# A fused two-layer kernel: the attention of the first layer in another order of work

## The chip, the cores and the metric

The kernel runs on one core of a Trainium2 chip. The metric is the device time of one execution in microseconds (us): lower is better. Engines are named PE (TensorE, the matmuls; PEld are its weight loads), DVE (VectorE), ACT (ScalarE), POOL (GpSimd) and SP (the queue that issues most transfers).

## The reference, cut to what matters

The input is x of 4 batches x 512 rows x 128. Layer 0 is attention and a mixture of experts, layer 1 a gated linear recurrence with its feed-forward parts. Each part reads the rows normalised to mean 0 and variance 1 and is added to them. The change touches attention, and of the tail its residual, norm and choice of experts:

```python
Q, K, V = (heads(WQ), heads(WK), heads(WV))          # 16 heads of 8
score = jnp.einsum('bhqd,bhkd->bhqk', Q, K) / jnp.sqrt(jnp.asarray(D_K, x.dtype))
score = score + mask                                 # causal
score = score - jnp.max(score, axis=-1, keepdims=True)
score = jnp.exp(score)
score = score / jnp.sum(score, axis=-1, keepdims=True)
out = jnp.einsum('bhqk,bhkd->bhqd', score, V)
out = out.transpose(0, 2, 1, 3).reshape(B, S, E)
return out @ WO
...
probs_full = jax.nn.softmax(xt @ Wr, axis=-1)        # 8 experts
topv, topi = jax.lax.top_k(probs_full, TOPK)         # 2 of them for each row
topv = topv / jnp.sum(topv, axis=-1, keepdims=True)
onehot = jax.nn.one_hot(topi, E, dtype=x.dtype)
rank = jnp.cumsum(onehot, axis=0)
keep = (rank <= capacity).astype(x.dtype) * onehot
...
x = x + _L0_attn_ref(_layernorm(x, axis=-1), L0_attn_WQ, L0_attn_WK, L0_attn_WV, L0_attn_WO)
x = x + _L0_ffn_ref(_layernorm(x, axis=-1), L0_ffn_Wr, L0_ffn_W1, L0_ffn_b1, L0_ffn_W2, L0_ffn_b2)
```

## The kernel before, in words

Attention works on groups of four heads of one batch: 4 batches (b) x 4 groups (g) are 16 groups, and loop step w treats group w. The lines are those of the functions printed below.

**Row scores.** To subtract a maximum, each group's scores are first computed with queries on the partitions: `row_scores(G, u)` makes ten blocks u of 128 queries x (4 heads x 128 keys) into three PSUM banks used in turn (`RING`, `row_free`); blocks 1, 4, 5 and 9 lie on the diagonal and take a second matmul that adds the mask. DVE's `row_max` reduces each (L1074) and so frees its bank. `minus_max` joins them and writes minus the maximum into two columns of MX for each head and tile (L1080 to L1082). PE turns MX (`turn_max`, L1687) and DVE adds it to the queries (`add_max`, L1088): QM.

**Key scores.** `key_scores(w, n)`, n = 0 to 11 (head n % 4; n // 4 is key tile 0, tile 1, or tiles 2 and 3) gives scores with keys on the partitions, the maximum already in them, in three more banks. ACT's `exp_unit` (L684) writes their exponentials to PT and frees the bank; POOL's `select` (L551) zeroes what is above the diagonal. `values(w, j)` multiplies key tile j with V, four heads on 32 columns of the array each (L1673), into bank 6. When all four tiles are in, ACT copies bank 6 to OG (`store_sums`, L691), PE turns it (`turn_out`, L1695) and DVE divides by the sums (`normalise`, L1096, L1097).

**One step.** Step w interleaves the row scores of group w + 1, the key scores of group w and the rest of group w - 1: key scores 10 and 11 and the values of tiles 1 (first visit), 2 and 3 (second visit); values(w, 0) are a third visit. Row scores 0 and 1 of group w + 2 come at the end of the step, ahead of the turned maxima of group w + 1. Key scores 8 and 9 of group w come before that turn. Each engine's order is written out by hand in its own block; all turns and small products share bank 7 in the order of `TURNS`.

**Queries and keys through DRAM.** They are held as a high and a low part in four planes of 8 rows (three products make up for single-precision ones; the fourth plane carries the maxima). When g = 0, PE makes the projections of batch b + 1 (`project`, L1632, L1633) in the ring banks, ACT rounds them (`round_halves`, L674), DVE takes the low parts (`make_halves`, L1064), and SP writes the planes to `qk_dram` (`store_planes`, six transfers) and loads them per group (`pad`: QS once, KP in four transfers, L409 and L418). Plane 4 is constant and stored ahead (`store_pads`, L384, L386). In DRAM a head is 4 planes x 8 rows.

**The tail of a batch** runs in the four steps of the next batch: heads turned (g = 0, L1701, ACT copy L702), product with WO, residual, mean and variance, POOL's root, normalisation on DVE (g = 1, L1707, L1110, L979 to L991), second turn and router logits (g = 2, L1715, L1721), choice of two experts (`choose`, `spread`, L1130 to L1144), ranks by matmul (g = 3), places and counts (`place`, `count`, L1159 to L1171). POOL scatters the normed rows to the experts' slots in DRAM (L537). The tail of the last batch stands by itself after the loop, in halves. The experts and layer 1 follow; the change leaves them as they are.

## Time and profile before

| | |
|---|---|
| median of 3 runs | 651.49 us (650.28 to 654.68) |
| the profiled execution | 651.65 us, of which the span from first to last instruction is 649.9 |
| PE busy | 577.0 us (89%), 3423 matmuls |
| PE weight loads | 440.7 us (68%) |
| DVE busy | 407.6 us (63%), 966 instructions |
| ACT busy | 325.8 us (50%), 567 |
| POOL busy | 172.5 us (27%), 185 |
| clock granted to PE | 0.964 of full speed in the mean |
| DRAM | 25.12 MB read, 16.78 MB written |
| chain that ended last | PE 62%, DVE 11%, issue 8%, ACT 6%, DMA 6% |

Matmuls overlap and their ends are modelled, so a busy PE is read by the starts of its instructions. The 16 attention steps take 27.8 to 209.7 us of the span, the experts about 236 to 320, layer 1 the rest.

### The profile page before, as it was taken

The page shows a single profiled execution, that of the slowest core. Times are in us where ns is not written, and L with a number is a line of the kernel's source. Part 1 is how long each engine was busy: PE and PEld are TensorE (multiplying, and loading weights), DVE is VectorE, ACT ScalarE, POOL GpSimd, SP SyncE. Part 2 cuts the span into 40 slices and gives each one's busy share as a digit, 9 for nine tenths or more (in the row PEclk, how much of TensorE's full clock was granted, in tenths as well). Part 3 has the DMA queues.
Part 4 walks back from the last instruction along what each step waited for, and adds up shares of the span by engine and source line. Part 5 has one row for each costly group of instructions (what it writes and reads, how often), then busy time and mean ns, then how long its engine had stood idle before and what let it go on. Part 6 is the DMA issues. An engine that isn't in the chain of part 4 may idle for free.

```text
span 649.9 us, 9448 instructions
## 1 busy us (share of the span) xinstructions
PE 577.0 (89%) x3423; PEld 440.7 (68%) x3423; DVE 407.6 (63%) x966; ACT 325.8 (50%) x567; POOL 172.5 (27%) x185
## 2 busy tenths in 40 slices
PE   7889989999998479979558688999999999998997
PEld 3556656556565369979435476678778878786866
DVE  6778688788885522533249986983769556762430
ACT  5756556556656116636216344752575256643451
POOL 6112122452542630000158623611300041001100
PEclk9999999999999679989879898999999999999999
DMA  4773242243110444764101100100000000000000
GB/s 131 229 252 105 75 131 66 82 146 98 54 45 2 133 148 128 211 204 126 48 25 32 29 6 1 33 1 1 1 18 1 0 1 18 0 1 2 17 1 16
DMA packets 44926, 42.51 MB, mean 65 GB/s; under 512 B 4176, under 2 KB 34384, under 8 KB 44880
## 3 DMA queue, kind: packets, MB, share of 16 engines
q1 hardware_dynamic: 42544, 37.44, 19.1%
q0 software_dynamic: 2048, 4.20, 2.2%
q8 instruction: 27, 0.44, 0.3%
q10 hardware_dynamic: 288, 0.28, 0.2%
q14 instruction: 19, 0.16, 0.1%
HBM read 25.12 MB, written 16.78 MB: 64 GB/s over the span
## 4 chain that ended last, share of the span: by engine, by line
PE 62%; DVE 11%; issue 8%; ACT 6%; DMA 6%; SPq 3%; POOL 2%; DVEq 0%; ACTq 0%; POOLq 0%
PE ps L1992 7%; PE ps L1645 5%; PE ps L1661 5%; PE ps L1673 5%; PE ps L2014 5%; PE ps L2095 4%; PE ps L2091 4%; PE ps L2092 4%; PE ps L1930 4%; PE ps L2015 4%; PE ps L2018 4%; DMA XS<-xs_dram 3%; PE ps L2008 2%; DVE pm L1074 2%; PE ps L1648 2%
## 5 line engine op out<-in xcount | busy, mean ns | idle before, releaser
L684 ACT ACTIVATE PT<-ps 128x384 f32<-128x384 f32 (+1 forms) x192 | 93.5, 529 | 69.6 <-PE ps L1661 65.0
L1074 DVE TENSOR_REDUCE pm<-ps 128x4 f32<-128x512 f32 x160 | 102.4, 683 | 10.0 <-PE ps L1645 9.4
L1645 PE MATMUL ps<-KP,QS 128*128 128x512 f32 x160 | 71.7, 452 | 7.7 <-DVEq L1067 2.5
L551 POOL TENSOR_SCALAR_AFFINE_SELECT PT<-PT 128x512 f32<-128x512 f32 x64 | 40.1, 638 | 128.0 <-ACT PT L684 126.6
L1661 PE MATMUL ps<-QM,KP 128*128 128x512 f32 (+3 forms) x256 | 69.2, 331 | 1.5 <-DVE QM L1088 1.1
L1661 PEld LDWEIGHTS ps<-QM,KP 128*128 128x128 f32 x256 | 43.8, 189 | 22.8 <-issue 13.4
L1645 PEld LDWEIGHTS ps<-KP,QS 128*128 128x128 f32 x160 | 29.8, 188 | 27.2 <-DVE pm L1074 10.7
L1444 DVE TENSOR_TENSOR_SCAN zero<-decay,OG 128x512 f32<-128x512 f32 x32 | 44.8, 1401 | 1.1
L1673 PE MATMUL ps<-PT,V 128*32 128x128 f32 (+3 forms) x512 | 44.6, 442 | 0.0
L526 POOL TENSOR_TENSOR rstd<-veps,mhalf 128x4 f32<-128x4 f32 x11 | 12.7, 1158 | 110.4 <-DVE veps L985 110.2
L814 ACT ACTIVATE HT<-ps,cols 128x640 f32<-128x640 f32 x32 | 25.4, 795 | 30.5 <-PE ps L1924 29.8
L875 ACT ACTIVATE hF<-ps,cols 128x512 f32<-128x512 f32 x16 | 11.0, 689 | 56.1 <-PE ps L2095 56.1
L1930 PE MATMUL ps<-W,HT 128*128 128x128 f32 x320 | 38.4, 275 | 0.0
L1930 PEld LDWEIGHTS ps<-W,HT 128*128 128x128 f32 x320 | 37.7, 192 | 0.0
L1439 DVE SCALAR_TENSOR_TENSOR OG<-ps,cols,vs 128x512 f32<-128x512 f32 x32 | 24.0, 749 | 18.1 <-ACT vs L854 17.8
L858 ACT ACTIVATE gs<-ps,half_bg 128x512 f32<-128x512 f32 x32 | 22.0, 688 | 25.7 <-PE ps L2018 24.6
L854 ACT ACTIVATE vs<-ps,cols 128x512 f32<-128x512 f32 x32 | 22.0, 688 | 18.9 <-PE ps L2018 18.7
L616 POOL DMA_INDIRECT G<-ys_dram,posG x8 | 7.6, 953 | 89.0 <-DMA ys_dram<-zero 86.8
L587 POOL DMA_INDIRECT G<-ys_dram,posG x24 | 29.3, 1222 | 6.8 <-issue 6.8
L1992 PEld LDWEIGHTS ps<-lwo,oT 128*128 128x128 f32 x256 | 29.1, 192 | 0.2
L1992 PE MATMUL ps<-lwo,oT 128*128 128x128 f32 x256 | 29.2, 275 | 0.0
L1953 PE MATMUL ps<-identr 128*128 128x512 f32 x47 | 15.2, 489 | 15.8 <-DMA G<-ys_dram,posG 13.1
(308 smaller groups left out, 1384.4 us busy)
## 6 DMA issues: line engine op xcount, KB each, us to landing
qk_dram<-HL SPq DMA_DIRECT2D x24, 256.0 KB
W<-in_eW SPq DMA_DIRECT2D x16, 256.0 KB
QS<-qk_dram SPq DMA_DIRECT2D x15, 256.0 KB
KP<-qk_dram SPq DMA_DIRECT2D x60, 64.0 KB
xs_dram<-zero SPq DMA_DIRECT2D x4, 640.0 KB, 3.5
XS<-xs_dram SPq DMA_DIRECT2D x8, 320.0 KB, 5.7
ys_dram<-zero SPq DMA_DIRECT2D x8, 320.0 KB, 2.9
whole_h_w<-in_h_w SPq DMA_DIRECT2D x2, 1024.0 KB, 8.8
```

Of the source, the lines that this page charges most:

```text
L551: g.affine_select(out=diag, in_=diag, pattern=[[0, 4], [1, P]], compare_op=ALU.is_ge, fill=0.0, base=0, channel_multiplier=-1).then_inc(se ...
L587: g.indirect_dma_start(out=G[:, b % 2, i, :], out_offset=None, in_=ys_dram, in_offset=bass.IndirectOffsetOnAxis(ap=posG[:, c:c + 1], axis= ...
L684: act.activation(PT[:, i, a:z], bank[ROWB + n % KEYB][:, 0:z - a], ACT.Exp, scale=float(DK) ** -0.5).then_inc(exp_done, 1)
L1074: v.tensor_reduce(pm[:, t, k, :], bank[n % ROWB].rearrange("p (i n) -> p i n", n=P), AXX, ALU.max).then_inc(row_free[n % ROWB], 1)
L1444: v.tensor_tensor_scan(st, decay[:, f:f + 1].to_broadcast([P, SEQ]), kv, 0.0, ALU.mult, ALU.add).then_inc(st_done, 1)
L1645: mm = pe.matmul(to, QS[:, G % 2, t * P:(t + 1) * P], KP[:, G % 3, k, :, :].rearrange("p i n -> p (i n)"), start=True, stop=t != k)
L1661: mm = pe.matmul(bank[ROWB + n % KEYB][:, at:at + SEQ - j * P], KP[:, w % 3, j, i, :], QM[:, w % 2, j * P:SEQ], start=True, stop=True)
L1673: mm = pe.matmul(bank[6][32 * i:32 * i + 32, j * P:SEQ], V[:, j * H + g * 4 + i, :], PT[:, i, OFF[j]:OFF[j + 1]], start=(j == 0), stop=(j ...
L1930: mm = pe.matmul(bank[4 + j // 4][:, (j % 4) * P:(j % 4 + 1) * P], HT[:, s, f, j * P:(j + 1) * P], W2[:, s, f, :], start=(f == 0 and j % 4 ...
L1992: mm = pe.matmul(bank[5][:, t * P:(t + 1) * P], src[:, f, t * P:(t + 1) * P], w[:, f, :], start=(f == 0 and t == 0), stop=(f == n - 1), sk ...
L2014: pe.matmul(to, high[n][:, cs], halves_of[:, 0, :], start=True, stop=False)
L2015: pe.matmul(to, low[n][:, cs], halves_of[:, 0, :], start=False, stop=False)
```

## The change

- PE: row scores 0 of group w + 1 move from the end of step w - 1 to the head of step w, row scores 1 behind the turn; key scores 8 and 9 of a group move behind the next turn of maxima, to 10 and 11. Values of tile 1 go to those of tiles 2 and 3. Logits move from late in the step to ahead of key scores 3, the turned heads ahead of key scores 6; row scores 7, 8 and 9 are one or two places earlier.
- ACT follows; rounding of the next batch and the copy of the turned heads stand ahead of exponentials 6 and 7. The norm of the tail is done here: x * rstd + nmr.
- DVE: the norm is gone; statistics and aggregates are two pieces, aggregates with nm = -mean; logits, choice, places and counts stand ahead of row maxima 7 or 8 and not behind `minus_max`; `normalise` follows row maximum 9.
- POOL: nmr = nm * rstd.
- SP: a pair of equal planes is one transfer (a source repeated); DRAM rows of the four planes interleave; stores of the constant planes, the three row loads and the clearing of the slots come later.

```diff
@@ _turns @@
+        if before >= 0 and g == 2:
+            at["logits", before] = len(at)
         if w:
             at["out", w - 1] = len(at)
-        if before >= 0 and g in (0, 2):
-            at[("turn", None, "logits")[g], before] = len(at)
+        if before >= 0 and g == 0:
+            at["turn", before] = len(at)
@@ SP @@
+                def twice(a, cs):
+
+                    to = qk_dram[b, a, :, :, cs, :].rearrange("h r c n -> (h r) c n")
+                    return sp.dma_start(to, HL[:, a, 0:1, :].bitcast(F32).to_broadcast([P, 2, SEQ]))
+
                 sp.wait_ge(parts, 2 * b + 1)
-                for c in (0, 2):
-                    sp.dma_start(qk_dram[b, 0, :, 8 * c:8 * c + 8, :], HL[:, 0, 0, :].bitcast(F32)).then_inc(q_planes, 16)
+                twice(0, slice(0, 3, 2)).then_inc(q_planes, 16)
...
             store_pads(0)
             store_planes(0)
             pad(1)
-            for b in range(1, NB):
-                store_pads(b)
-            for i, n in enumerate(("bo", "b2", "w3_s")):
-                sp.dma_start(rows[:, i, :], d[n].partition_broadcast(P)).then_inc(w1_in, 16)
             for G in range(2, NW):
                 if G % NG == 3 and G // NG + 1 < NB:
                     store_planes(G // NG + 1)
                 pad(G)
-                if G in (2, 3, 4, 5):
-                    clear_slots(G - 2)
+                if G - 1 in range(1, NB):
+                    store_pads(G - 1)
+                elif G == 5:
+                    for i, n in enumerate(("bo", "b2", "w3_s")):
+                        sp.dma_start(rows[:, i, :], d[n].partition_broadcast(P)).then_inc(w1_in, 16)
+                if G in (3, 4, 5, 6):
+                    clear_slots(G - 3)
@@ POOL @@
                     rsqrt(varA, rsA, before + 1)
+                    g.wait_ge(rsA, 2 * before + 1)
+                    g.tensor_tensor(nmr[:, :], nm[:, :], rstd[:, :], ALU.mult).then_inc(rsA, 1)
@@ ACT @@
+            def tail_norm(b):
+                act.wait_ge(rsA, 2 * b + 2)
+                act.wait_ge(scattered, b * 16 * TOPK * TB)
+                for t in range(TB):
+                    ins = act.activation(xn[:, t, :], X[:, b * TB + t, :], ACT.Identity, scale=rstd[:, t:t + 1],
+                                         bias=nmr[:, t:t + 1])
+                ins.then_inc(xnA, 1)
...
                 if w:
-                    exp_unit(w - 1, 10)
-                    exp_unit(w - 1, 11)
+                    for n in range(8, 12):
+                        exp_unit(w - 1, n)
...
                 exp_unit(w, 5)
+                if g == 0 and b + 1 < NB:
+                    round_halves(b + 1)
+                if b and g == 0:
+                    take_turn("turn", b - 1, OT[:, :])
                 exp_unit(w, 6)
                 exp_unit(w, 7)
-                if g == 0 and b + 1 < NB:
-                    round_halves(b + 1)
-                exp_unit(w, 8)
-                if b and g == 0:
-                    take_turn("turn", b - 1, OT[:, :])
-                exp_unit(w, 9)
+                if b and g == 1:
+                    tail_norm(b - 1)
@@ DVE @@
                     row_max(w + 1, 1)
                     row_max(w + 1, 2)
+                    row_max(w + 1, 3)
                 if b and g == 1:
                     add()
                 if b and g == 3:
                     ranks()
                 if rows_next:
-                    row_max(w + 1, 3)
                     row_max(w + 1, 4)
                 if b and g == 1:
                     stats_()
                 if rows_next:
                     row_max(w + 1, 5)
                     row_max(w + 1, 6)
-                    row_max(w + 1, 7)
-                if w:
-                    normalise(w - 1)
-                if rows_next:
-                    row_max(w + 1, 8)
-                    row_max(w + 1, 9)
-                    minus_max(w + 1)
-                if g == 0 and b + 1 < NB:
-                    make_halves(b + 1)
                 if b and g == 1:
-                    norm()
+                    variances()
                 if b and g == 2:
                     take_logits()
+                if rows_next:
+                    row_max(w + 1, 7)
+                if b and g == 2:
                     choose()
                     spread()
                 if b and g == 3:
                     place()
                     count()
+                if rows_next:
+                    row_max(w + 1, 8)
+                    row_max(w + 1, 9)
+                if w:
+                    normalise(w - 1)
+                if rows_next:
+                    minus_max(w + 1)
+                if g == 0 and b + 1 < NB:
+                    make_halves(b + 1)
@@ PE @@
-            row_scores(1, 0)
-            row_scores(1, 1)
             for w in range(NW):
...
+                if rows_next:
+                    row_scores(w + 1, 0)
                 turn_max(w)
                 if w:
+                    key_scores(w - 1, 8)
+                if rows_next:
+                    row_scores(w + 1, 1)
+                if w:
+                    key_scores(w - 1, 9)
                     key_scores(w - 1, 10)
                 if rows_next:
                     row_scores(w + 1, 2)
                 if w:
                     key_scores(w - 1, 11)
-                    values(w - 1, 1)
...
+                if b and g == 2:
+                    logits(b - 1)
                 key_scores(w, 3)
+                if rows_next:
+                    row_scores(w + 1, 7)
+                    row_scores(w + 1, 8)
                 if w:
+                    values(w - 1, 1)
                     values(w - 1, 2)
                     values(w - 1, 3)
                 if rows_next:
-                    row_scores(w + 1, 7)
+                    row_scores(w + 1, 9)
                 key_scores(w, 4)
-                if rows_next:
-                    row_scores(w + 1, 8)
                 key_scores(w, 5)
                 if w:
                     turn_out(w - 1)
-                if rows_next:
-                    row_scores(w + 1, 9)
                 if g == 0 and b + 1 < NB:
                     project(b + 1)
                 values(w, 0)
+                if b and g == 0:
+                    turn_heads(b - 1)
                 key_scores(w, 6)
                 key_scores(w, 7)
-                if b and g == 0:
-                    turn_heads(b - 1)
-                if b and g == 2:
-                    logits(b - 1)
-                key_scores(w, 8)
-                if w + 2 < NW:
-                    row_scores(w + 2, 0)
-                key_scores(w, 9)
-                if w + 2 < NW:
-                    row_scores(w + 2, 1)
```

## Rows read from the trace of the kernel before

**Rows 1.** Busy time of each engine by stretch, with its length, granted clock and DMA share.

```profile
core 0: us, PE busy (x) PEld busy (x) DVE busy (x) ACT busy (x) POOL busy (x), PEclk, DMA share, GB/s
27.80:39.74 11.94, 9.86 (x43) 5.57 (x42) 8.53 (x16) 6.60 (x13) 1.28 (x2) 1.00 0.69 225
...
49.72:59.72 10.00, 10.00 (x72) 6.38 (x71) 8.21 (x17) 6.35 (x14) 2.50 (x5) 1.00 0.35 120
...
69.72:83.08 13.36, 12.38 (x79) 7.39 (x78) 8.87 (x18) 8.19 (x18) 2.73 (x5) 1.00 0.15 44
83.08:95.46 12.38, 11.49 (x79) 7.25 (x79) 10.70 (x29) 6.61 (x14) 3.27 (x5) 1.00 0.55 168
95.46:106.59 11.13, 11.13 (x84) 7.68 (x83) 9.47 (x27) 7.08 (x15) 2.74 (x5) 1.00 0.18 47
106.59:117.32 10.73, 10.72 (x85) 6.65 (x84) 9.73 (x33) 6.23 (x14) 2.27 (x4) 1.00 0.16 50
117.32:131.44 14.12, 12.94 (x79) 7.38 (x78) 10.27 (x25) 8.19 (x18) 7.55 (x10) 1.00 0.35 98
...
165.42:176.70 11.28, 10.94 (x75) 6.63 (x74) 9.74 (x24) 7.29 (x16) 6.79 (x10) 1.00 0.24 71
...
188.79:199.17 10.38, 10.38 (x81) 7.12 (x79) 8.89 (x20) 6.37 (x13) 2.45 (x5) 1.00 0.01 2
```

**Rows 2.** Instructions in order of time, stretch 2: start, length, engine, idle before.

```profile
53.63 0.39 PE L1645 MATMUL ps<-KP,QS 128*128 128x512 f32 x1
53.86 0.39 PE L1661 MATMUL ps<-QM,KP 128*128 128x512 f32 x1
54.17 0.86 PE L1673 MATMUL ps<-PT,V 128*32 128x256 f32 x16
54.96 0.50 PE L1645 MATMUL ps<-KP,QS 128*128 128x512 f32 x1
55.30 0.34 PE L1661 MATMUL ps<-QM,KP 128*128 128x384 f32 x1
...
55.89 0.60 PE L1695 MATMUL ps<-const,OG 128*128 128x128 f32 x4
...
56.90 0.16 PEld L1673 LDWEIGHTS ps<-PT,V 128*32 128x32 f32 x8 [0.37 <-issue]
...
57.89 0.64 PEld L1661 LDWEIGHTS ps<-QM,KP 128*128 128x128 f32 x4 [0.84 <-issue]
...
58.92 0.30 PEld L1661 LDWEIGHTS ps<-QM,KP 128*128 128x128 f32 x2 [0.27 <-ACT PT L684]
```

**Rows 3.** DVE in order of time, end of stretch 2.

```profile
56.53 0.26 DVE L1096 RECIPROCAL rden<-ps 128x16 f32<-128x16 f32 x1 [0.34 <-PE ps L1695]
...
57.03 1.28 DVE L1074 TENSOR_REDUCE pm<-ps 128x4 f32<-128x512 f32 x2
...
58.97 0.19 DVE L1082 SCALAR_TENSOR_TENSOR MX<-mx,MX 128x16 fp32r<-128x16 f32 x1
```

**Rows 4.** In order of time, stretch 0: SP's issue of the key load, PE's wait.

```profile
32.31 2.48 SPq L418 DMA_DIRECT2D KP<-qk_dram  x4
...
38.74 0.47 PE L1645 MATMUL ps<-KP,QS 128*128 128x512 f32 x1 [1.67 <-DMA KP<-qk_dram]
```

**Rows 5.** In order of time, end of stretch 4: ACT and PE's weight load.

```profile
82.39 0.64 ACT L702 ACTIVATE OT<-ps 128x512 f32<-128x512 f32 x1
82.50 0.19 PEld L1645 LDWEIGHTS ps<-KP,QS 128*128 128x128 f32 x1 [1.13 <-DVEq L1067]
```

**Rows 6.** In order of time, stretch 5: PE's weight load and DVE.

```profile
91.12 0.19 PEld L1645 LDWEIGHTS ps<-KP,QS 128*128 128x128 f32 x1 [1.27 <-DVE pm L1074]
...
94.81 1.47 DVE L991 TENSOR_SCALAR xn<-X,mv,rstd 128x128 f32<-128x128 f32 x4
```

**Rows 7.** ACT in order of time, the norm of batch 1 ahead of attention.

```profile
16.33 1.65 ACT L709 ACTIVATE O<-X,VR,rstd 128x128 f32<-128x128 f32 x4
```

**Rows 8.** Busy time by stretch, columns as in rows 1: choice (L1130 to L1144), places and counts.

```profile
105.87:107.72 1.85, 1.85 (x14) 1.61 (x12) 1.60 (x16) 1.20 (x3) 0.27 (x1) 1.00 0.04 9
116.67:118.55 1.88, 1.88 (x17) 1.61 (x21) 1.67 (x12) 1.35 (x4) 0.64 (x1) 1.00 0.00 0
```

More of the change, by code:

```diff
@@ L1112, in stats_, with variances @@
                     v.wait_ge(tp_free, TURNS["wo", b] + 1)
-                    ln_stats(xt, link, varA)
-                def norm():
-                    v.wait_ge(scattered, b * 16 * TOPK * TB)
-                    ln_apply(xt, lambda t: xn[:, t, :], rsA, b + 1, xnA)
+                    v.sem_inc(v_paced, 1)
+                    for t in range(TB):
+                        ins = v.bn_stats(stats[:, t, :], xt(t))
+                    link(ins)
+                def variances():
+                    v.sem_inc(v_paced, 1)
+                    for t in range(TB):
+                        ins = v.bn_aggr(mv[:, t, :], stats[:, t, :])
+                    link(ins)
+                    v.tensor_scalar(nm[:, :], mv[:, :, 0], -1.0, None, ALU.mult)
+                    v.tensor_scalar(veps[:, :], mv[:, :, 1], EPS, None, ALU.add).then_inc(varA, 1)
                 def take_logits():
@@ L1172, in count @@
                     assert link.k == NLT, link.k
-                return add, stats_, norm, take_logits, choose, spread, ranks, place, count
+                return add, stats_, variances, take_logits, choose, spread, ranks, place, count
             make_halves(0)
@@ L2186, in shape_constants @@
     at += 8
-    plane = i % 32 // 8
+    plane = i % 4
     c[:, at] = np.where(plane == 1, -1.0, 0.0)
```

45 lines of the change are left out of this document (25 added, 20 removed).

## The prediction

> **What bounds the kernel now.** I read the busy times by stretch first. A stretch runs from the start of one group's turned maxima to the next; there are sixteen, 0 to 15, from 27.80 to 209.65 us of the span. A stretch without tail work (1 to 3) takes 10.00, and TensorE is busy in all of it; VectorE has 8.21, ScalarE 6.35 [rows 1]. Those with tail work take 10.4 to 14.1, and there TensorE is idle for up to 1.2 while VectorE is nearly full: 10.70 of 12.38 in stretch 5 [rows 1]. So the plain stretches are TensorE's, and the others are those of the handoffs between TensorE and VectorE. The clock granted to TensorE is 1.00, the 2.4 GHz level, in all of them.
>
> Then the order of time inside a plain stretch [rows 2]. Neighbouring 512-column matmuls start 0.23 apart (53.63, 53.86). A visit to the 32-column value products breaks this: 53.86 to 54.17 is 0.31, so entering costs 0.08. The turn at 55.89 moves 4 x 128 columns in two passes: 0.33 plus 0.27 for the last, so a pass of 128 columns is 0.11. The visit at 54.17 holds 256 + 128 columns in two passes, 0.66, and its follower starts at 54.96, 0.79 later: 0.13. The next step is 0.34 and not 0.23: 0.11. A visit thus costs about 0.3 beside its products. The last row is a wait of a key product for ScalarE, 0.17 in starts.
>
> **The change, part by part.** Times are in us; t is the start of a turn of maxima, T that of row scores 9.
>
> Values in two visits: tile 1 joins tiles 2 and 3, one visit fewer in stretches 1 to 15: 0.3 each. Key scores 8 to 11 move behind the turn, so the ScalarE wait of 0.17 has exponentials ahead of it and should go. A plain stretch is then 10.00 - 0.30 - 0.17 = 9.54. What could be late next is the turn itself. From T, TensorE has row scores 9 (0.34 + 0.23), keys 4 and 5 (0.36), the turn of the sums to the next visit (0.53), tile 0 (57.89 - 56.90 = 0.99), keys 6 and 7 (0.45), row scores 0 (0.23): the turn of maxima is due at T + 3.13, and T is at t + 6.41. VectorE has: row scores 9 landed at T + 0.63, maximum 0.60, the sums normalised (0.5, as 56.53 to 57.03), then 0.85 to the last write of MX (58.31 to 59.16) [rows 3], with the sums there at T + 1.42: MX at T + 2.8. Slack 0.3, no wait. The long visit (0.3 + 1.32 of products + row step, 1.80 in all) costs ScalarE and VectorE only idle time: they have 3.6 and 1.8 to spare [rows 1].
>
> Stretch 0. Before, its end waits 1.67 for the key load, issued from 32.31 on (2.48) and landed at 38.74 [rows 4], behind six pad stores and three row loads on SP's queue. Moved behind, the load waits only for the first QM. Row scores 1 of group 1 now come behind the turn, so t is 0.55 earlier, 27.25 (two matmuls of 0.23 and their handoff), and QM, 0.6 after the turn and 0.68 long, is done at 28.5; the four issues end at 31.4; with the same 3.95 to land, 35.35. TensorE meanwhile: VectorE's nine maxima at 0.60 [rows 3] end at 33.95, row scores 9 start at 32.2 when their bank is free, keys 0.8, projections 1.8, tile 0, keys 6 and 7 and row scores 0: the next turn at 36.45, for 39.74. The load is 1 ahead. Gain 3.3, with 0.55 of it the earlier start. Bounds: if it lands as late after the issue of the first pads as now, 38.7, the gain is 0.6; if landing were instant, still 3.3. I take 3.3, nearest to the row of the same transfer. The paired plane stores save SP two issues a batch (0.6 each), and what waits for planes is 2 or more ahead in stretches 4, 8 and 12: nothing. As the trace has no such store of 256 rows, its bounds are 0 and, if it takes twice the 0.6 and lands as much later, 0.6 once, before stretch 0, where the key load has 0.5 to spare.
>
> Stretches 4, 8, 12 (heads turned; 4 and 8 also project). Now TensorE waits 1.13 of weight-load idle for the subtraction of the low halves and the turn waits for the copy of the turned heads (0.64) [rows 5]. After: the rounding stands ahead of exponentials 6 and 7 and of that copy, so both halves are free by T + 4.9, ahead of row scores 1. Work: 9.54 + 1.93 (projections) + 0.34 (heads) and 0.15 of wait for the copy: 11.95; without projections 10.0. Against 13.36, 14.12, 11.28: -1.41, -2.17, -1.28.
>
> Stretches 5, 9, 13 (WO product, statistics). VectorE's norm, 1.47, goes to ScalarE, and statistics are cut in two. TensorE: 9.54 + 0.80. VectorE has row maxima 0 to 3 done at t + 3.3, the sum 3.4 to 4.0, maximum 4 at 4.6, statistics to 5.5, maximum 5 at 6.1: row scores 8 wait for that bank, due at t + 5.4, start at 6.15. Wait 0.75, where row scores now wait 1.27 of idle for the same bank [rows 6]. The aggregates (0.9) then fall under the value visit. Period 11.1 for 12.38, and for 12.1 in the other two: -3.3 in the three.
>
> Stretches 6, 10, 14 (second turn, logits). This is the bill. The four norms on ScalarE take 1.65 as in the first part of the kernel [rows 7], between exponential 7 and 8: key 11 waits for exponential 8, 1.04 behind its slot, and all after it. With 0.38 (turn) and 0.78 (logits): 11.75. VectorE: the choice, 1.85 [rows 8], now lies between maxima 7 and 8, so maximum 9 ends at t + 10.5 and MX at 11.75, just with it. I take 11.8, 11.8 and 11.7, for 11.13, 11.14 and 10.38: +2.65. In these stretches the choice used to stand behind MX, under TensorE's next work.
>
> By the Trainium skill (ScalarE: Activation LUTs, Rules for kernel authors), additions and products should be on VectorE, not ScalarE. The rows say so too per instruction, 0.37 against 0.41 apart, but it is the engine with less to do that gets them; followed as it stands it would keep the norm on VectorE: stretches 6, 10 and 14 would lose their 1.04 and stretches 5, 9 and 13 gain at most 1.47 again.
>
> Stretches 7, 11 (ranks, places). Places and counts, 1.88 [rows 8], also move ahead of maxima 8 and 9: with 0.3 for the ranks MX is at t + 10.35, TensorE is ready at 9.9. Period 10.4 for 10.73: -0.67 in both. Stretch 15 has no rows; QM is no longer late and keys 8 and 9 of group 14 come on top: -0.3.
>
> Plain stretches 1 to 3: 3 x 0.45 = -1.35.
>
> **Sum.** -3.3 - 1.35 - 4.86 - 3.3 + 2.65 - 0.67 - 0.3 = -11.1. What follows attention (scatters on POOL, expert loads on SP behind the last values) waits for semaphores of its end and moves with it whole. My walk leaves out small handoffs: by the same terms stretch 7 now would be 10.00 + 0.37, and it takes 10.73. I give back 0.1 a tail stretch, 1.0. The profiled execution took 651.65 (span 649.9 and 1.75 around it), 0.16 above the median of 651.49: 651.65 - 10.1 = 641.5. I leave the 0.16 in.
>
> **Rivals.**
> 1. VectorE becomes the bound of all tail stretches. Its busy time there is 9.5 to 10.7, all of its tail work now stands ahead of MX, and the long visit idles it. If each of the eleven tail stretches is 0.5 longer than above, the gain is 5.6: 646. For: the +0.65 above is of this kind. Against: in stretches 5, 9, 13 it loses 1.47. Chance 0.18.
> 2. Slower. The turn waits in every stretch: MX now stands behind the normalising, that behind the turned sums, these behind the copy of the sums, and that behind the whole value visit, which was done 5 ahead before. Slack 0.3. A chain 1.4 longer than I walked would cost 1.1 x 15 = 16.5: 658. It decides from 1.0 past the slack on. Against it: each link is a row of its own, and none was late. Chance 0.06.
> 3. The start doesn't move: the key load still lands at 38.7 because paired stores and pads share the transfer engines (share 0.69 in stretch 0 [rows 1]). Gain 8.4 - 1.0: 644.2. Chance 0.16.
> 4. The change hardly does what it says: tail work is only moved about, and what one stretch wins the next pays. Stretches 5 to 6 and 7 to 8 speak for it, the idle TensorE of 1.2 in stretch 4 against it. Gain 2: 649.6. Chance 0.08.
>
> TensorE's tail. After attention the granted clock falls to 1.2 GHz while only small products run, and again for shorter times between the experts; where those fall is shifted by the change, which may give or take about 2. By the Trainium skill (TensorE: Matmul & The Clock Gate, Single matmul latency) the fixed part of a matmul is 166 ns at the high clock; a visit with two switches would cost 0.33 by it, and the visits would give 5.0 where the rows give 0.30 x 15 = 4.5.
>
> **The numbers.** Forecast 0.52, rivals 0.18, 0.06, 0.16, 0.08. The forecast's own range is 638 to 644.5: 2 for the clock, 1.5 for the handoffs. To hold 8 in 10 it reaches over rivals 1 and 3 on the slow side, and a walk without the allowance and with a lucky clock on the other: 637 to 648. A difference of 1% is 6.5 (about what a measurement here tells from none). Faster by more, below 645.0: all of the forecast but 0.04, three quarters of rival 3, a third of rival 1: 0.48 + 0.12 + 0.06 and 0.03 of surprises, 0.69. Slower by more: rival 2 and as much again for what I don't see, 0.08. The rest, 0.23, within 1%.
>
> **What would show it.** Two PE visits in a stretch, one of about 1.5; plain stretches at 9.5; the second turn near 36.5 with no DMA ahead of it; no wait for the low halves; in stretches 6, 10, 14 a TensorE wait of about 1 for ScalarE behind four norms; ten or more small VectorE instructions ahead of maximum 8. Plain stretches at 10 or a turn that waits for MX in them would make the forecast wrong; tail stretches of 12 and more would be rival 1.

## The result and the profile after

| set of runs | before, median | changed, median | ratio, 95% interval |
|---|---|---|---|
| 1 (9 and 9 runs) | 652.13 | 647.07 (645.49 to 648.89) | 0.9924 [0.9904, 0.9943] |
| 2 (`changed_again`) | 653.39 | 644.71 (644.00 to 645.55) | 0.9874 [0.9858, 0.9891] |
| 3 (`changed_third`) | 653.45 | 645.14 (644.71 to 645.20) | 0.9875 [0.9855, 0.9894] |
| 4 (`changed_fourth`) | 652.14 | 644.70 (643.31 to 645.16) | 0.9876 [0.9856, 0.9897] |

The result that the prediction was made for is set 1: 5.1 us faster, where 10.1 were forecast. The other sets are the same kernel on other occasions, with gains of 7.4 to 8.7. The ratio is of the fast executions (one of the kernel before in set 4, at 825.86, was slow) and is not the quotient of the two medians. The profiled execution of set 1 took 648.14 (span 646.4); it is profile 1 below, and sets 2 to 4 gave profiles 2 to 4. Its stretches, in the view of [rows 1]:

```profile
core 0: us, PE busy (x) PEld busy (x) DVE busy (x) ACT busy (x) POOL busy (x), PEclk, DMA share, GB/s
27.19:36.74 9.55, 9.31 (x39) 5.14 (x38) 8.69 (x16) 5.97 (x11) 0.64 (x1) 1.00 0.43 133
36.74:46.38 9.64, 9.64 (x71) 6.58 (x70) 7.96 (x16) 6.37 (x14) 2.49 (x4) 1.00 0.91 320
65.63:77.63 12.00, 11.90 (x79) 7.50 (x78) 9.39 (x19) 8.40 (x18) 2.49 (x4) 1.00 0.47 171
77.63:89.16 11.53, 10.74 (x78) 7.53 (x79) 10.16 (x27) 6.42 (x14) 3.70 (x6) 1.00 0.41 143
89.16:101.17 12.01, 11.27 (x83) 7.74 (x82) 9.90 (x34) 8.51 (x20) 2.49 (x4) 1.00 0.16 44
101.17:111.65 10.48, 10.27 (x85) 6.80 (x85) 10.05 (x29) 6.46 (x15) 2.49 (x4) 1.00 0.19 52
111.65:124.36 12.71, 12.10 (x78) 7.49 (x78) 9.50 (x19) 8.03 (x17) 6.58 (x8) 1.00 0.43 141
158.59:170.27 11.68, 10.38 (x74) 6.86 (x75) 8.09 (x17) 6.85 (x15) 6.43 (x8) 1.00 0.21 67
181.80:193.81 12.01, 11.04 (x83) 7.57 (x81) 9.82 (x33) 8.51 (x20) 2.49 (x4) 1.00 0.00 1
```

The rows are stretches 0, 1, 4, 5, 6, 7, 8, 12 and 14. Every stretch with VectorE's tail work has TensorE idle for 0.1 to 1.0; in stretch 12 it is idle for 1.3, with no engine full. The same view of the second profile of the same kernel, stretches 8 and 12:

```profile
111.92:123.94 12.02, 11.91 (x78) 7.52 (x78) 9.48 (x19) 8.05 (x17) 6.58 (x8) 1.00 0.47 151
157.99:168.31 10.32, 10.21 (x74) 6.88 (x74) 8.09 (x17) 6.85 (x15) 6.42 (x8) 1.00 0.26 77
```

All lengths, from turn of maxima to turn of maxima (the third and fourth profiles agree with the second within 0.05):

| stretch | before | forecast | profile 1 | profile 2 |
|---|---|---|---|---|
| 0 | 11.94 | 9.2 | 9.55 | 9.55 |
| 1, 2, 3, each | 10.0 | 9.54 | 9.63 | 9.63 |
| 4 | 13.36 | 11.95 | 12.00 | 12.01 |
| 5, 9, 13 | 12.38, 12.10, 12.09 | 11.1 | 11.53, 11.73, 11.53 | 11.52, 11.52, 11.51 |
| 6, 10, 14 | 11.13, 11.14, 10.38 | 11.8, 11.8, 11.7 | 12.01, 12.00, 12.00 | 12.01, 12.03, 12.02 |
| 7, 11 | 10.73, 10.74 | 10.4 | 10.48, 10.49 | 10.46, 10.50 |
| 8 | 14.12 | 11.95 | 12.71 | 12.02 |
| 12 | 11.28 | 10.0 | 11.68 | 10.32 |
| sum, 0 to 14 | 171.37 | 161.1, and 1.0 of allowance | 166.62 | 164.37 |

So the miss has two parts: 2.3 beyond the allowance that every profile has (most of it in stretches 5, 9, 13, then 6, 10, 14, then 0 and 12), and 2.3 in stretches 8, 12 and 9 that only the first has. What attention gained arrived: in profile 1 its last exponential ends 5.55 earlier. That profile shows only 3.5 at the end. Of the 2.0 in between, 0.4 are lost by the middle of the program (410 us), and 1.6 where a part of layer 1 ran at the lower granted clock: VectorE's instructions lead those of the kernel before by 5.1 ahead of it and by 3.5 behind it. The first row is 3.4 us of profile 1, the second the same stretch of work before:

```profile
615.90:619.30 3.40, 3.40 (x9) 2.72 (x9) 0.65 (x2) 0.55 (x1) 0.00 (x0) 0.50 0.02 5
```

```profile
621.20:624.60 3.40, 3.40 (x16) 2.72 (x15) 1.07 (x2) 1.27 (x2) 0.00 (x0) 1.00 0.02 5
```

The figure behind the five engines is the clock: 0.50, the 1.2 GHz level, against 1.00. 9 matmuls are recorded there instead of 16. This is the 2 either way that the prediction left for the tail. The median of the set, 5.06, is near attention's 5.55.

**The long visit** came as drawn: in stretch 2 of profile 1 (order of time, TensorE, as [rows 2]) tiles 1, 2 and 3 are one block of 1.50, and the turn at its end does not wait for MX.

```profile
50.75 0.77 PE L1676 MATMUL ps<-KP,QS 128*128 128x512 f32 x2
51.01 0.19 PEld L1676 LDWEIGHTS ps<-KP,QS 128*128 128x128 f32 x1 [0.30 <-DVE pm L1097]
...
51.45 1.50 PE L1704 MATMUL ps<-PT,V 128*32 128x384 f32 x24
...
52.88 0.50 PE L1676 MATMUL ps<-KP,QS 128*128 128x512 f32 x1
```

**The key load** of group 2 (as [rows 4]) is issued from 29.07 instead of 32.31 and nothing waits for it; TensorE's next turn of maxima is at 36.74.

```profile
29.07 2.46 SPq L428 DMA_DIRECT2D KP<-qk_dram  x4
...
31.58 0.59 SPq L388 DMA_DIRECT2D qk_dram<-zero  x1
32.21 0.43 SPq L390 DMA_DIRECT2D qk_dram<-low_h_w  x1
```

**The bill of stretch 6**: ScalarE's norm between exponentials 7 and 8 of group 5, 1.64 long (forecast 1.65), and the wait of key product 11 behind it, 0.93 of weight-load idle (forecast 1.04).

```profile
89.71 1.64 ACT L730 ACTIVATE xn<-X,nmr,rstd 128x128 f32<-128x128 f32 x4
...
91.25 1.24 ACT L697 ACTIVATE PT<-ps 128x384 f32<-128x384 f32 x3
91.77 0.30 PEld L1692 LDWEIGHTS ps<-QM,KP 128*128 128x128 f32 x2 [0.93 <-ACT PT L697]
```

**The turn of maxima and MX**, end of stretch 6. VectorE's last write of MX ends 0.15 before the turn, and the turn starts 0.51 after the matmul ahead of it:

```profile
100.66 0.40 PE L1676 MATMUL ps<-KP,QS 128*128 128x512 f32 x1
100.83 0.19 DVE L1105 SCALAR_TENSOR_TENSOR MX<-mx,MX 128x16 fp32r<-128x16 f32 x1
...
101.17 0.63 PE L1718 MATMUL ps<-const,MX 128*128 128x128 f32 x4
```

In stretches 1 to 3 that step is 0.23, and MX is done 0.37 to 0.39 before the turn. So at the end of stretch 6 the turn waits for MX, by 0.3. It does so in every profile of the changed kernel at the ends of stretches 6, 7, 10, 11 and 14 (MX done 0.14 to 0.15 before it, a step of 0.5 to 0.7). At the ends of stretches 4, 8 and 12 MX is done 1.0 to 2.8 before, and the turn waits for ScalarE's copy of the turned heads instead (a step of 0.50).

**Stretch 12 of profile 1**: TensorE's block of values starts at 163.66 and its last products are recorded in order and on time; yet the copy of the sums (L704) starts at 166.63, 1.74 after the last of them, and all that waits for TensorE is late with it.

```profile
163.66 1.50 PE L1704 MATMUL ps<-PT,V 128*32 128x384 f32 x24
...
164.19 0.96 POOL L548 DMA_INDIRECT xs_dram<-xn,posS  x1 [0.30 <-issue]
...
165.15 0.65 POOL L562 TENSOR_SCALAR_AFFINE_SELECT PT<-PT 128x512 f32<-128x512 f32 x1
...
166.63 0.60 ACT L704 ACTIVATE OG<-ps 128x512 f32<-128x512 f32 x1 [2.83 <-PE ps L1704]
166.67 0.69 DVE L1097 TENSOR_REDUCE pm<-ps 128x4 f32<-128x512 f32 x1 [1.70 <-PE ps L1679]
```

The same place in profile 2. From the start of the block to the copy it is 1.56 instead of 2.97, with GpSimd's scatter in the same place:

```profile
163.09 1.50 PE L1704 MATMUL ps<-PT,V 128*32 128x384 f32 x24
...
163.59 0.96 POOL L548 DMA_INDIRECT xs_dram<-xn,posS  x1 [0.30 <-issue]
...
164.57 0.64 POOL L562 TENSOR_SCALAR_AFFINE_SELECT PT<-PT 128x512 f32<-128x512 f32 x1
164.65 0.60 ACT L704 ACTIVATE OG<-ps 128x512 f32<-128x512 f32 x1 [1.44 <-PE ps L1704]
165.28 0.69 DVE L1097 TENSOR_REDUCE pm<-ps 128x4 f32<-128x512 f32 x1 [0.89 <-PE ps L1679]
```

### The profile page after: what moved, and what is told of

The parts are those of the page before. It is cut to its first block, busy times and chain, and to the rows that moved or that the text cites. A ratio compares the mean times of both kernels' runs of the same rounds, so it can differ in the third digit from the quotient of the medians.

```text
span 646.4 us, 9449 instructions
## 1 busy us (share of the span) xinstructions
PE 574.1 (89%) x3423; PEld 445.8 (69%) x3423; DVE 405.6 (63%) x957; ACT 329.4 (51%) x579; POOL 173.2 (27%) x188
## 4 chain that ended last, share of the span: by engine, by line
PE 65%; DVE 11%; issue 8%; ACT 7%; DMA 5%; POOL 2%; SPq 2%; DVEq 0%; ACTq 0%; POOLq 0%
PE ps L2021 7%; PE ps L1704 5%; PE ps L1676 5%; PE ps L1692 5%; PE ps L2043 5%; PE ps L2124 4%; PE ps L2120 4%; PE ps L2044 4%; PE ps L2121 4%; PE ps L1959 4%; PE ps L2047 4%; DMA XS<-xs_dram 3%; DVE pm L1097 2%; PE ps L2037 2%; PE ps L1679 2%
## 5 line engine op out<-in xcount | busy, mean ns | idle before, releaser
L697 ACT ACTIVATE PT<-ps 128x384 f32<-128x384 f32 (+1 forms) x192 | 91.5, 526 | 33.0 <-PE ps L1692 29.2
L1676 PE MATMUL ps<-KP,QS 128*128 128x512 f32 x160 | 67.7, 436 | 4.4 <-DVE pm L1097 2.0
L1692 PE MATMUL ps<-QM,KP 128*128 128x512 f32 (+3 forms) x256 | 65.4, 329 | 2.3 <-ACT PT L697 2.3
L1704 PE MATMUL ps<-PT,V 128*32 128x128 f32 (+3 forms) x512 | 41.5, 439 | 0.0
```

Source lines behind the costliest of these rows:

```text
L697: act.activation(PT[:, i, a:z], bank[ROWB + n % KEYB][:, 0:z - a], ACT.Exp, scale=float(DK) ** -0.5).then_inc(exp_done, 1)
L1676: mm = pe.matmul(to, QS[:, G % 2, t * P:(t + 1) * P], KP[:, G % 3, k, :, :].rearrange("p i n -> p (i n)"), start=True, stop=t != k)
L1692: mm = pe.matmul(bank[ROWB + n % KEYB][:, at:at + SEQ - j * P], KP[:, w % 3, j, i, :], QM[:, w % 2, j * P:SEQ], start=True, stop=True)
L1704: mm = pe.matmul(bank[6][32 * i:32 * i + 32, j * P:SEQ], V[:, j * H + g * 4 + i, :], PT[:, i, OFF[j]:OFF[j + 1]], start=(j == 0), stop=(j ...
```

## The experiments

**1. `scatters_moved`** (changed kernel, GpSimd's program):

```diff
                 select(w, 0)
                 if at == 0 and before > 0:
-                    scatter(before - 1, range(2, 4))
+                    scatter(before - 1, range(0, 5))
+                if at == 1 and before > 0:
+                    scatter(before - 1, range(7, 8))
                 if at == 1 and before >= 0:
                     rsqrt(varA, rsA, before + 1)
...
                 select(w, 1)
                 if at == 0 and before > 0:
-                    scatter(before - 1, range(4, 6))
+                    scatter(before - 1, range(5, 7))
                 select(w, 2)
-                if at == 0 and before > 0:
-                    scatter(before - 1, range(6, 8))
-                if at == 3 and before >= 0 and w + 1 < NW:
-                    if before == 0:
-                        g.wait_ge(zeroed, 64)
-                    scatter(before, range(0, 2))
+                if at == 3 and before == 0:
+                    g.wait_ge(zeroed, 64)
```

> The changed kernel with the token scatters of GpSimd (8 for each of batches 0 and 1) moved away from the value visit: five stand behind the first select of stretches 8 and 12, two behind the second select, one behind the first select of the stretch that follows; none stands between the third select (5 us into the stretch, where the value visit begins) and the first. Theory: the values of tiles 2 and 3 are finished 0.85 and 1.3 us late in stretches 8 and 12 because GpSimd issues scatters at that moment. Then the copy of the sums starts 0.34 after the last value product there too, stretch 8 falls from 12.71 to about 12.0 and stretch 12 from 11.68 to about 10.0, all others stay, and the time is 2.4 below the changed kernel: 644.7. Rival: the delay is due to something else in these stretches (the copy of the values to V, the loads on SP, the heads): both stretches stay as they are and the time is 647. A third outcome: the hold follows the scatters to where they stand now, and the turn of the heads or the first key products of the next stretch are late by 0.8 to 1.3.

Measured 644.98, ratio 0.9894 [0.9869, 0.9919]; stretches 8 and 12 took 12.04 and 10.30. That looked like a proof, and was none: the comparison was with one profile of another occasion.

**2. `norm_on_vector`** (the core of the edit; GpSimd's product for `nmr` goes too):

```diff
                 exp_unit(w, 7)
-                if b and g == 1:
-                    tail_norm(b - 1)
...
                 if g == 0 and b + 1 < NB:
                     make_halves(b + 1)
+                if b and g == 1:
+                    norm()
```

> The changed kernel with the tail's norm back on VectorE behind the maxima (its place before the change), the rest of the change as it is. Theory of the prediction: ScalarE's four norms hold up key product 11 by 1.04, so stretches 6, 10 and 14 fall from 12.0 to about 11.0; the norm, 1.47 on VectorE, runs under the turn and the key products 8 to 11, which now stand ahead of everything that waits for VectorE, so that at most some 0.3 a stretch comes back in row maxima: the time is 2.2 to 3.1 below the changed kernel, 644.4. Rival: VectorE is the bound of the tail stretches, its 1.47 is paid in full (maximum 0, QM and the row maxima are late, key product 0 waits): -1.04 + 1.47, three times, 648.4.

Measured 642.50, 0.9864 [0.9833, 0.9895]. Stretch 6 takes 11.11, stretch 5 is unchanged at 11.53: the norm on VectorE costs nothing there. On the medians alone the interval overlaps that of experiment 1; experiment 6 sets the two kernels apart. And stretches 8 and 12 take 12.03 and 10.30 with every scatter where the change has it, which spoke against experiment 1's theory.

```profile
89.81:100.92 11.11, 11.00 (x83) 7.76 (x82) 10.32 (x37) 7.24 (x16) 2.50 (x4) 1.00 0.17 48
111.41:123.44 12.03, 11.93 (x78) 7.51 (x78) 9.46 (x19) 7.95 (x17) 6.58 (x8) 1.00 0.45 139
156.59:166.89 10.30, 10.20 (x74) 6.87 (x75) 8.09 (x17) 6.84 (x15) 6.42 (x8) 1.00 0.24 75
```

**3. `before_later_pads`** (the kernel before, SP's queue):

```diff
-            for b in range(1, NB):
-                store_pads(b)
-            for i, n in enumerate(("bo", "b2", "w3_s")):
-                sp.dma_start(rows[:, i, :], d[n].partition_broadcast(P)).then_inc(w1_in, 16)
             for G in range(2, NW):
...
                 pad(G)
-                if G in (2, 3, 4, 5):
-                    clear_slots(G - 2)
+                if G - 1 in range(1, NB):
+                    store_pads(G - 1)
+                elif G == 5:
+                    for i, n in enumerate(("bo", "b2", "w3_s")):
+                        sp.dma_start(rows[:, i, :], d[n].partition_broadcast(P)).then_inc(w1_in, 16)
+                if G in (3, 4, 5, 6):
+                    clear_slots(G - 3)
```

> The kernel before with one part of the change alone: the pad stores of batches 1 to 3 and the three row loads stand behind the loads of groups 2 to 5 on SP's queue. Theory: the key load of group 2 waited behind them, its 1.67 of TensorE idle goes, stretch 0 falls from 11.94 to 10.3, and that passes to the end: 650.5 for 652.1 of the kernel before. Rival: the load is late for its transfer, not for its place: stretch 0 keeps 11.5 or more and the time is 652. Moved stores that get in the way of the loads of groups 3 to 5 would show as a wait of TensorE for a key load in stretches 1 to 3.

Measured 651.92, 0.9992 [0.9969, 1.0015]: nothing. The load is issued at 29.53 and no wait for it is left, but row scores 0 start at 38.96 instead of 38.74. They now wait for VectorE, whose subtraction of the low halves waits for ScalarE's rounding (L675), late behind the exponentials. Order of time, end of stretch 0:

```profile
37.52 1.09 ACT L675 ACTIVATE HL<-ps 128x512 fp32r<-128x512 f32 x2
...
38.16 1.53 DVE L1065 TENSOR_TENSOR HL<-ps,HL 128x512 fp32r<-128x512 f32 x2 [2.80 <-ACT HL L675]
38.96 0.19 PEld L1646 LDWEIGHTS ps<-KP,QS 128*128 128x128 f32 x1 [1.36 <-DVEq L1068]
```

**4. `before_pads_rounding`**: the same with the rounding between exponentials 5 and 6.

```diff
                 exp_unit(w, 5)
+                if g == 0 and b + 1 < NB:
+                    round_halves(b + 1)
                 exp_unit(w, 6)
                 exp_unit(w, 7)
-                if g == 0 and b + 1 < NB:
-                    round_halves(b + 1)
```

> The kernel before with two parts of the change: the later pads and row loads, and the rounding of the next batch's halves ahead of exponentials 6 and 7. With the pads alone the key load landed 4.9 earlier, yet TensorE then waited 1.36 for the subtraction of the low halves, behind a rounding that stood late on ScalarE. Theory: the two waits were one behind the other, and only both edits together free stretch 0: it falls from 11.94 to 10.3, and stretches 4 and 8, which waited 1.13 for the same subtraction, fall by 0.5 to 1.1 each; with 1.6 from stretch 0 the time is 3 below the kernel before: 649.1. Rival: the rounding delays exponentials 6 and 7 by its 1.2 and with them the values of tile 1, and nothing is gained: 652.

Measured 648.60, 0.9926 [0.9908, 0.9945]: stretch 0 takes 10.31, stretches 4 and 8 take 12.45 and 13.23 for 13.36 and 14.12. Pads alone bring 0, pads and rounding 4.8 on the median and 3.4 in the three stretches: two waits in series, and the first hid the second. The rounding alone was not run; the 0.9 each in stretches 4 and 8, which wait for no key load, are its own.

**5. `three_visits`** (changed kernel, TensorE's order):

```diff
                     key_scores(w - 1, 11)
+                    values(w - 1, 1)
...
                 if w:
-                    values(w - 1, 1)
                     values(w - 1, 2)
```

> The changed kernel with value tile 1 back in a visit of its own behind key product 11, the rest as it is. Theory: a visit to the 32-column products costs 0.3 beside its products, so plain stretches rise from 9.64 to 9.94, all fifteen by 0.3, and the time is 4.5 above the changed kernel: 651.6. Rival: the stretches are set by ScalarE's exponentials and the handoffs of VectorE, and a visit is hidden: plain stretches stay under 9.75 and the time is below 649. In stretches 8 and 12 only tiles 2 and 3 are then near the scatters; if these hold up whatever value product is in flight, the excess stays there.

Measured 652.27, 1.0001 [0.9986, 1.0016]: with this one edit the whole gain is gone. Attention is 7.2 longer than in profile 2. Two rows, stretches 1 and 6:

```profile
36.92:46.83 9.91, 9.91 (x72) 6.51 (x70) 8.16 (x16) 6.38 (x14) 2.50 (x4) 1.00 0.87 311
90.78:103.73 12.95, 11.56 (x84) 7.70 (x82) 9.96 (x34) 8.92 (x20) 2.69 (x5) 1.00 0.16 41
```

A plain stretch pays 0.29. The Trainium skill (TensorE: Matmul & The Clock Gate, Single matmul latency) gives 166 ns as the fixed part of one matmul at the high clock and says nothing of switches; as an estimate from it two would be 0.33, and the 0.29 is near that. But stretches 6, 7, 10, 11 and 14 pay 0.9 to 1.0. There the turn of maxima waits longer for MX:

```profile
103.70 0.42 PEld L1718 LDWEIGHTS ps<-const,MX 128*128 128x128 f32 x4 [1.11 <-DVE O L1120]
103.73 0.63 PE L1718 MATMUL ps<-const,MX 128*128 128x128 f32 x4 [0.76 <-DVE MX L1105]
```

The early visit puts its 0.66 of products and its 0.3 ahead of row scores 3. From maximum 3 on VectorE's maxima come 0.8 to 0.95 later, in plain stretches (profile 2 against this one, stretch 2) as in stretch 6. In a plain stretch the shorter second visit gives 0.66 back before row scores 9, and VectorE follows them; in the five others the choice or the places stand between the maxima, the turn waited for MX already, and MX comes 0.93 later in stretch 6.

**6. `both`** (edits 1 and 2), and **7. `changed_again`**, the changed kernel itself.

> The changed kernel with the two edits that gained by themselves: the norm back on VectorE behind the maxima, and the scatters away from the value visit. If they are independent, stretches 6, 10 and 14 take 11.1, stretches 8 and 12 take 12.0 and 10.3, and the time is 641.7, with little spread among the runs (1 or less, for the 3 of the changed kernel), because no execution has a value visit held up. Rival: with the norm on VectorE no value visit was held up in the one profile (12.03 and 10.30), so the scatters' place is worth nothing on top: 642.5 and the spread stays 2 to 3.

> The changed kernel itself, for one more profile and more times on the chip of the others. Theory: the hold-up of the values of tiles 2 and 3 in stretches 8 and 12 is no fixed cost, it strikes in some executions when scatters are issued during the value visit: the runs are spread over 645 to 649, and the profile shows stretches 8 and 12 with 12.0 to 12.7 and 10.3 to 11.7, not the same values as in the first. Rival: it is a fixed cost of this order of instructions: 12.7 and 11.7 again, and the low runs of 645.5 have another cause.

Measured 641.38, 0.9825 [0.9808, 0.9842], and 644.71, 0.9874. Stretches 8 and 12 of `changed_again` take 12.02 and 10.32 with the scatters in the value visit: the first profile's hold-up is no fixed cost of the program. The intervals of the two do not overlap.

**8. `both_choice_behind`** (`choose()`, `spread()`, `place()`, `count()` from ahead of `row_max(w + 1, 8)` to behind `minus_max(w + 1)`):

```diff
                 if rows_next:
                     row_max(w + 1, 7)
-                if b and g == 2:
-                    choose()
-                    spread()
-                if b and g == 3:
-                    place()
-                    count()
...
                     norm()
+                if b and g == 2:
+                    choose()
+                    spread()
+                if b and g == 3:
+                    place()
+                    count()
```

> The kernel with both edits, and besides the choice of experts (stretches 6, 10, 14) and the places and counts (7, 11) back behind the maxima of the next group, where they stood before the change. Theory: ahead of row maximum 8 they cost what stretches 6, 10, 14 and 7, 11 take over the sum of TensorE's work in them (11.11 for 9.64 + 0.38 + 0.78; 10.49 for 9.64 + 0.37): 0.3 and 0.4 each, so stretches 6, 10, 14 fall to 10.8 and 7, 11 to 10.1, and the time is 1.5 below the kernel with both edits. Rival: behind the maxima they delay row maximum 0 and QM of the next stretch by 1.85 and key product 0 waits: nothing is gained, or up to 0.5 a stretch is lost.

Measured 646.92, 0.9897 [0.9880, 0.9914]: 5.5 slower than `both`. Attention is 3.2 longer in its profile, which is of its slowest execution (650.21); the rest of the 5.5 is not accounted for. Stretches 6, 7 and 8:

```profile
89.59:100.43 10.84, 10.84 (x84) 7.87 (x83) 9.14 (x24) 6.97 (x15) 2.50 (x4) 1.00 0.15 49
100.43:111.88 11.45, 10.83 (x86) 6.95 (x84) 10.16 (x33) 6.36 (x14) 2.49 (x4) 1.00 0.16 47
111.88:125.08 13.20, 12.79 (x79) 7.51 (x77) 10.63 (x27) 8.31 (x18) 7.24 (x9) 1.00 0.39 123
```

The stretch that is relieved gains 0.3 (11.12 to 10.84), the next loses 1.0 to 1.2 (10.47 to 11.45; 12.03 to 13.20). So ahead of MX is the better place for this work in the changed order. What the move was worth in the order before was not run.

**9. `changed_third`, `scatters_again`**: the changed kernel and edit 1 side by side.

> The changed kernel once more. In its second profile the values of stretches 8 and 12 were not held up (12.02 and 10.32), with every scatter where it stood in the first (12.71 and 11.68). Theory A: the hold-up strikes in some executions or in some sessions on the chip; if it strikes here, one of the two stretches is above 12.3 or 10.6 and the time is near 647, otherwise all stretches are within 0.05 of the second profile and the time is 644 to 645. Theory B (the scatters' place decides): this kernel is slower than the one with moved scatters in the same call by 2.

> The changed kernel with the scatters away from the value visit, beside the changed kernel on the same chip. If the scatters' place causes the hold-up, it is faster by 2 than the changed kernel here; if the hold-up comes by chance and is absent here, both take the same, 644 to 645, within 0.5; if it comes by chance whatever the place, this kernel shows it too (8 above 12.3 or 12 above 10.6).

Measured 645.14, 0.9875 [0.9855, 0.9894], and 645.26, 0.9880 [0.9858, 0.9903]; stretch 12 takes 10.31 and 10.35. In three of the four profiles of the changed kernel the scatters stand in the value visit and nothing is held up, and moving them gains nothing: their place alone does not cause the hold-up. Whether it takes part in one cannot be told, as none came again.

**10. `both_again`, `both_stats_later`**:

```diff
+                if rows_next:
+                    row_max(w + 1, 5)
                 if b and g == 1:
                     stats_()
                 if rows_next:
-                    row_max(w + 1, 5)
                     row_max(w + 1, 6)
```

> The kernel with the norm on VectorE and the scatters moved, as the measure for the next one on the same chip. It took 0.9825 of the kernel before; expected again 0.980 to 0.985, with stretches 5, 9 and 13 at 11.52.

> The kernel with both edits, and the four statistics of the tail (0.87 on VectorE) behind row maximum 5 in place of ahead of it. Theory: in stretches 5, 9 and 13 row scores 8 wait 0.8 to 1.2 for the bank of row scores 5, because the sum, maximum 4 and the statistics stand ahead of its maximum; the wait was forecast as 0.75 and the stretches came out 0.43 above the forecast. With the statistics behind it the maximum ends 0.87 earlier, row scores 9 are the next to need a bank and come 1.5 later, and the stretches fall from 11.52 to 10.7 or 10.9: 2 to 2.5 in all, 639. Rival: the 0.43 is TensorE's own work or a wait for ScalarE, and the bank of row 6 is then the one that is late: the stretches fall by less than 0.3 and the time by less than 1.

Measured 642.16, 0.9829 [0.9811, 0.9848], and 640.85, 0.9809 [0.9785, 0.9833]. Stretches 5, 9 and 13 fall from 11.5 to 10.6, and TensorE is busy in all of them:

```profile
77.67:88.30 10.63, 10.63 (x79) 7.47 (x79) 10.07 (x28) 6.42 (x14) 3.51 (x5) 1.00 0.47 155
```

In profile 1 TensorE waited 1.22 for the maximum of row scores 5, behind sum, maximum 4 and statistics:

```profile
81.31 0.69 DVE L1133 TENSOR_TENSOR X<-ps,X 128x512 f32<-128x512 f32 x1 [0.30 <-PE ps L1738]
...
81.92 0.68 DVE L1097 TENSOR_REDUCE pm<-ps 128x4 f32<-128x512 f32 x1
...
82.52 0.86 DVE L1138 BATCH_NORM_STATS2 stats<-X 128x6 f32<-128x128 f32 x4
...
83.42 1.29 DVE L1097 TENSOR_REDUCE pm<-ps 128x4 f32<-128x512 f32 x2
84.16 0.19 PEld L1676 LDWEIGHTS ps<-KP,QS 128*128 128x128 f32 x1 [1.22 <-DVE pm L1097]
```

In the kernel with the statistics later that wait is 0.33:

```profile
83.16 0.86 DVE L1132 BATCH_NORM_STATS2 stats<-X 128x6 f32<-128x128 f32 x4
83.29 0.19 PEld L1677 LDWEIGHTS ps<-KP,QS 128*128 128x128 f32 x1 [0.33 <-DVE pm L1091]
```

Attention is 2.7 shorter (first to last turn of maxima, 161.62 to 158.95). The medians differ by 1.3, and their intervals overlap: for the whole time this gain is not shown.

**11. `changed_fourth`, `norm_and_stats`**: the changed kernel again, and edits 2 and 10 with the scatters as in the change.

> The changed kernel a fourth time. Its first nine runs had a median of 647.07 (0.9924 of the kernel before), the next two sets 644.71 and 645.14 (0.9874, 0.9875), and only the first profile has values held up in stretches 8 and 12. If the level of the first set belongs to the program, some set must show it again: 647 and a hold-up of 0.7 to 1.4 here. If it belonged to that session, this one has 644.5 to 645.5, a ratio of 0.985 to 0.990, and no copy of the sums later than 0.4 after the last value product.

> The changed kernel with the norm back on VectorE and the statistics behind row maximum 5, the scatters where the change has them. As the place of the scatters made no difference beside the changed kernel (645.3 and 645.1), this version should equal the one that also moves them, 640.9 and 0.981, with stretches 5, 9, 13 at 10.6, 6, 10, 14 at 11.1, 8 at 12.0 and 12 at 10.3. Rival: with VectorE's row maxima earlier the value visit and the scatters meet and stretches 8 or 12 are held up: 12.7 or 11.7, 643.

Measured 644.70, 0.9876 [0.9856, 0.9897], and 641.19, 0.9827 [0.9799, 0.9854]. Stretches 8 and 12 take 12.02 and 10.30, and 12.04 and 10.30. Stretches 9 and 10 of the second take 10.84 and 11.42, for 10.61 and 11.12 with the scatters moved: the inverse roots on GpSimd, and with them the norm, wait for the scatters. There moving them is worth 0.5 in the profile. The lowest ratio is that of `both_stats_later`, 0.9809, below the change's 0.9874 to 0.9876 by 0.7%, with intervals that stay apart; from `norm_and_stats` and `both` its interval does not part.

## Why the forecast of the gain was twice too large

The sign, the mechanism and most terms were right, and the time fell inside the range; the size was wrong by 5. The step that failed is the walk through the tail stretches: it took the start of each link there from VectorE's and ScalarE's chains without the handoffs, and set only 1.0 aside for these. The runs show 3.3 in their place (profile 2): 1.3 in stretches 5, 9 and 13 (a gain of 2.0 for the 3.3 forecast), 0.8 in 6, 10 and 14 (a loss of 3.4 for 2.65), 0.35 in stretch 0, 0.3 in 12, 0.3 in the plain ones and 0.3 in the rest. In set 1 another 2.3 came on top that no term held, and their cause is open. The time lies in the range because that reached over rival 1, not because the forecast was near.

**Right, within 0.1 a stretch.** The visit: 0.3 forecast; the way back costs 0.29. Plain stretches 9.54, measured 9.63; row scores 9 come at t + 6.50 for 6.41, behind small waits as the 0.30 of weight-load idle ahead of the long visit, and from there to the turn it is 3.14 for 3.13. Stretch 4 (11.95; 12.0): the wait for the low halves is gone, and that for the turned heads is left, 0.27 where the prediction had 0.15. Stretches 7 and 11 (10.4; 10.5): MX is done at t + 10.33 for 10.35, the turn waits for it as forecast, and the handoff of 0.15 was left out. In plain stretches the turn does not wait for MX, so rival 2 did not come: MX is done 0.37 before it, of which 0.15 is the handoff, so the slack is 0.22 for 0.3. In stretches 6, 7, 10, 11 and 14 there is none, and that is why one more visit ahead of row scores 3 costs three times as much there.

**Stretch 0.** Forecast 9.2, measured 9.55. Row scores 9 start at 32.32 for 32.2, and from them to the projections it is 0.93 for 0.8; from there the parts take what the walk gave them, and the turn is at 36.74 for 36.45. The attribution was incomplete. The prediction gave 3.3 to the key load's place in SP's queue. Alone it is worth nothing; it needs the rounding ahead of exponentials 6 and 7, which I had credited to stretches 4 and 8 only. That the sum survived is luck: the change happens to do both.

**Stretches 5, 9, 13: the first mis-sized term, 0.42 each.** The prediction named the wait, "row scores 8 wait for that bank", as 0.75. The sum of the residual started at t + 3.68 instead of 3.4, every link after it kept that 0.3, and row scores 8 came at t + 6.53 instead of 6.15: 0.38 of the 0.42 is there. Moving the statistics behind maximum 5 takes away 0.9, which confirms that the stretch hangs on this chain. The prediction also had maximum 5 behind the statistics as given, and never asked what they were ahead of.

**Stretches 6, 10, 14: right in kind, 0.2 to 0.3 short.** ScalarE's norm holds up key product 11: with the norm on VectorE they take 11.1 for 12.0. The prediction had MX "just with" the turn at t + 11.75; it is done at t + 11.87, and the turn waits for it and starts 0.14 later. The 1.47 on VectorE that its move was to save was worth nothing (stretches 5, 9 and 13 keep their 11.53 with the norm back), for it ran under the turn and key products 8 to 11, which the change itself had put there. The Trainium skill (ScalarE: Activation LUTs, Rules for kernel authors) would have such products on VectorE; the runs side with it by 2.7 (attention of `norm_on_vector` against profile 2), though not for the price of an instruction (0.37 and 0.41 apart), but for what waits behind each engine.

**Rivals.** Rival 3 did not come, as nothing waits for the key load. Rival 1 (tail stretches 0.5 longer, VectorE's fault, 646) is the nearest to what came. Without the hold-up the eleven are longer by 0.24 on average, most of it VectorE's in 5, 9 and 13 and ScalarE's in 6, 10 and 14.

**The other 2.3.** In profile 1 stretch 8 lost 0.69, stretch 9 0.21 and stretch 12 1.36 against profile 2, to a hold-up that no term could hold. Sets 2 to 4 are lower than set 1 by 1.9 to 2.4 on the median, as much as the hold-up. Two of set 1's nine executions (645.49, 645.61) lie near the level of sets 2 to 4, seven at 646.9 to 648.9, so I take most executions of set 1 to have had it. The clock does not account for it: the mean granted clock is 0.960 to 0.962 in set 1 and 0.959 to 0.962 in sets 2 to 4. That they had the hold-up is argued, not shown: set 1 has one profile. With sets 2 to 4 as the measure the gain was 7.4 to 8.7 for 10.1 forecast, and the walk's own error is 2.3 beyond its allowance.

## What to carry to other kernels

When a wait goes away, ask for the same instruction which other condition it would meet next: here the key load hid the low halves, and the single edit gained nothing. Work of a second engine belongs where it stands ahead of nothing that the bound engine needs soon: four statistics one place later were worth 0.9 a stretch, a norm behind the maxima was free, while 1.85 of choice there cost 1.0 in the next stretch. These prices are of single profiles. And before an excess in one profile is explained, take a second profile of the same program.

## What was not expected of the hardware

In profile 1 of the changed kernel TensorE's value products are recorded on time, and all that waits for them (the copy of the sums and the maximum of row scores 9) is released 0.7 late in stretch 8 and 1.4 late in stretch 12, within 0.1 of each other. The copy starts 1.06 and 1.74 after the last product's recorded start, where it is 0.34 to 0.40 in these two stretches of the 15 other profiles of this case. In stretch 9 of the same profile the sum of the residual starts 0.51 after the last product with WO, where it is 0.31 in profile 2. GpSimd issued a scatter during each of the three groups of products, as it does at the same places in profile 2 without a hold-up. What it is stays open.
